# Products of the unit matrix, read by nobody, in TensorE's pauses at three borders of stages

## The reference

```python
x = x + L0_attn(L0_cond(x))    # diagonal state space kernel, 32 heads of causal attention
x = x + L0_ffn(L0_cond2(x))    # low rank adapter per labeler, octonion ternary gate/up/down
x = x + L1_attn(L1_cond(x))    # gathered adapters, 4 heads of sigmoid attention
x = x + L1_ffn(L1_cond2(x))    # top-2 and sparsemax mixtures of rank-16 experts
```

## Time and profile before

| | us |
|---|---|
| median of 3 runs | 2157.1 |
| the runs | 2154.85, 2158.34, 2157.1 |
| the profiled execution | 2158.86 |
| its span, first to last instruction | 2157.1 |
| PE busy | 2108.3 (98%) |
| POOL, DVE, ACT busy | 1255.8, 1338.5, 730.9 |
| mean granted clock of PE | 0.991 |

### The profile page before, as it was taken

The page is one execution under the profiler, slowest core; times in us unless marked ns, Lnnn a source line. Parts: engine busy times, 40 slices in busy tenths (PEclk is TensorE's granted clock), DMA queues, the critical chain, the costliest instruction groups (busy, mean ns, idle before and its releaser), DMA issues. The chain is left out here.

```text
span 2157.1 us, 36235 instructions
## 1 busy us (share of the span) xinstructions
PE 2108.3 (98%) x11876; PEld 1822.5 (84%) x11876; DVE 1338.5 (62%) x2465; ACT 730.9 (34%) x1454; POOL 1255.8 (58%) x1315
## 2 busy tenths in 40 slices
PE   7899999999999998999999999999999999999999
PEld 5788888989888897889898898989887777778887
DVE  7656565665656567665666566566666666654444
ACT  5233232332323233332323233232333645443332
POOL 3587585766758575767758576775844732114220
PEclk9999999999999999999999999999999999999999
DMA  7411112111111210311111211111112200001110
GB/s 238 149 50 40 40 42 65 49 39 39 39 39 40 66 50 30 88 40 40 39 39 39 68 49 39 39 39 39 40 61 78 92 14 0 0 0 40 39 39 19
DMA packets 92036, 107.57 MB, mean 50 GB/s; under 512 B 5569, under 2 KB 71777, under 8 KB 90817
## 3 DMA queue, kind: packets, MB, share of 16 engines
q1 hardware_dynamic: 90689, 102.53, 15.7%
q0 software_dynamic: 1280, 4.20, 0.7%
HBM read 100.79 MB, written 5.94 MB: 49 GB/s over the span
## 5 line engine op out<-in xcount | busy, mean ns | idle before, releaser
L215 PE MATMUL psum<-yc,wh 128*128 128x512 f32 x904 | 363.4, 402 | 9.5 <-DVE yc L1499 5.0
L216 PE MATMUL psum<-yc,wh 128*128 128x512 f32 x904 | 354.6, 392 | 0.0
L217 PE MATMUL psum<-yc,wh 128*128 128x512 f32 x904 | 354.2, 392 | 0.0
L1359 DVE TENSOR_TENSOR resid<-psum,resid 128x512 f32<-128x512 f32 x248 | 171.3, 691 | 148.5 <-PE psum L217 144.3
L215 PE MATMUL psum<-kept,yc 128*128 128x256 f32 x896 | 255.9, 286 | 1.7 <-DVE v_tok L1309 1.0
L941 POOL TENSOR_TENSOR wh<-wh_f,wh 128x256 fp32r<-128x256 f32 x256 | 191.8, 760 | 110.9 <-ACT wh L907 109.0
L217 PE MATMUL psum<-kept,yc 128*128 128x256 f32 x896 | 253.5, 283 | 0.0
L216 PE MATMUL psum<-kept,yc 128*128 128x256 f32 x896 | 253.4, 283 | 0.0
L215 PEld LDWEIGHTS psum<-yc,wh 128*128 128x128 f32 x904 | 171.6, 190 | 43.3 <-DVE yc L1499 5.8
L217 PEld LDWEIGHTS psum<-yc,wh 128*128 128x128 f32 x904 | 170.9, 189 | 36.6
L941 POOL TENSOR_TENSOR wh<-raw,wh 128x256 fp32r<-128x256 f32 x192 | 142.2, 741 | 96.2 <-ACT wh L907 96.2
(11 more groups left out here) (355 smaller groups left out, 4818.5 us busy)
## 6 DMA issues: line engine op xcount, KB each, us to landing
raw<-in_attn_w SPq DMA_DIRECT2D x96, 512.0 KB, 4.8
wo_f<-in_attn_w SPq DMA_DIRECT2D x31, 512.0 KB, 4.0
hankel<-kernel_rows SPq DMA_DIRECT2D x32, 256.0 KB, 4.7
resid<-in_xT SPq DMA_DIRECT2D x4, 1024.0 KB, 9.8
outT<-wide SPq DMA_DIRECT2D x16, 256.0 KB, 2.6
kept_f<-in_l_w SPq DMA_DIRECT2D x3, 1024.0 KB, 5.5
work_f<-in_oct_w SPq DMA_DIRECT2D x4, 680.0 KB, 4.1
resid<-in_xT SPq DMA_DIRECT2D x4, 512.0 KB, 6.1
```

Of the source, the lines that this page charges most:

```text
L215: pe.matmul(out, w[0], x[0], start=start, stop=False)
L216: pe.matmul(out, w[0], x[1], start=False, stop=False)
L217: return pe.matmul(out, w[1], x[0], start=False, stop=stop)
L1359: dve.tensor_tensor(part, psum[:, 5 + (GH + m) % 3, :], part, ALU.add).then_inc(tail_free, 1)
```

## The change

A helper issues `count` float32 products of the unit matrix with the first 256 columns of the constants (themselves never written after their load) into a PSUM bank that nobody reads before it is written anew. Each product is two matmul instructions of 256 columns. It is called six times, at the end of PE's program ahead of a border and at the start of the one behind it: 2 and 5 products at border 1, 2 and 3 at border 2, 2 and 4 at border 3. The first call has a wait ahead of it, for copies of ACT out of the bank that it writes. All else in the diff passes `consts` on.

```diff
+def keep_warm(pe, bank, consts, ident, count):
+
+    for _ in range(count):
+        pe.matmul(bank[:, 0:2 * P], ident, consts[:, 0:2 * P], start=True, stop=True)
...
             convolve(QUARTERS - 1, NCB - 1)
+            pe.wait_ge(comp_copied, 2 * CROWS)
+            keep_warm(pe, psum[:, 6, :], consts, const("ident"), 2)
...
             pe.sem_inc(prod_done, 2)
+            keep_warm(pe, psum[:, 7, :], consts, const("ident"), 5)
             product(0, 0, "P1", fresh=0, start=True)
...
                 for m in range(KC):
                     end_output(i, m)
+            keep_warm(pe, psum[:, 0, :], consts, const("ident"), 2)
...
                 pe.sem_inc(x_used, KC)
+                keep_warm(pe, psum[:, 3, :], consts, const("ident"), 3)
                 with pe.Fori(0, NT) as tile:
...
                     down_product(SLOTS - 2)
                     down_product(SLOTS - 1)
+                keep_warm(pe, psum[:, 2, :], consts, const("ident"), 2)
...
                 pe.sem_inc(x_used, KC)
+                keep_warm(pe, psum[:, 3, :], consts, const("ident"), 4)
                 with pe.Fori(0, NT) as tile:
```

More of the change, by code:

```diff
@@ L240, in build_program @@
         s4d_and_convolution(nc, t, sb, sem, const, consts, resid, psum, kernel_rows, later, hw, v_tok, combos)
-        attention(nc, t, sb, sem, overlaid, const, mm3, resid, psum, kept_raw, kept, hw, v_tok, combos)
+        attention(nc, t, sb, sem, overlaid, const, consts, mm3, resid, psum, kept_raw, kept, hw, v_tok, combos)
         attn.close()
         later["ranks_raw"], later["ranks"] = overlaid(ctx, "ranks", [P, 4, TT])
-        octonion_ffn(nc, t, sb, sem, overlaid, const, mm3, resid, psum, kept_raw, kept, later)
-        layer_one(nc, t, sb, sem, const, mm3, resid, psum, kept_raw, kept, later)
+        octonion_ffn(nc, t, sb, sem, overlaid, const, consts, mm3, resid, psum, kept_raw, kept, later)
+        layer_one(nc, t, sb, sem, const, consts, mm3, resid, psum, kept_raw, kept, later)
+def keep_warm(pe, bank, consts, ident, count):
+    for _ in range(count):
+        pe.matmul(bank[:, 0:2 * P], ident, consts[:, 0:2 * P], start=True, stop=True)
 def wait_apart(engine, semaphore, value, passed):
@@ L971, in load_values, with attention @@
                          .rearrange("g p n -> (g p) n")).then_inc(self.raw_in[p], 16)
-def attention(nc, t, sb, sem, overlaid, const, mm3, resid, psum, kept_raw, kept, hw, v_tok, combos):
+def attention(nc, t, sb, sem, overlaid, const, consts, mm3, resid, psum, kept_raw, kept, hw, v_tok, combos):
     QUADS, HALFTOK = HEADS // 4, 2 * TT
@@ L1790, in gather_adapters, with octonion_ffn @@
                                     ).then_inc(later["gathered"], 16)
-def octonion_ffn(nc, t, sb, sem, overlaid, const, mm3, resid, psum, kept_raw, kept, later):
+def octonion_ffn(nc, t, sb, sem, overlaid, const, consts, mm3, resid, psum, kept_raw, kept, later):
     ctx = ExitStack()
@@ L2357, in _, with layer_one @@
                     down_product(SLOTS - 1)
-def layer_one(nc, t, sb, sem, const, mm3, resid, psum, kept_raw, kept, later):
+                keep_warm(pe, psum[:, 2, :], consts, const("ident"), 2)
+def layer_one(nc, t, sb, sem, const, consts, mm3, resid, psum, kept_raw, kept, later):
     NM = 2
```

## The result

| | kernel before | changed kernel |
|---|---|---|
| median of the runs, us | 2157.6 (2154.85 to 2161.7, 20 runs) | 2154.3 (2153.6 to 2157.4, 20 runs) |
| ratio, 95% interval | | 0.9986 [0.9979, 0.9992] |
| profiled execution (span), us | 2158.86 (2157.1) | 2155.34 (2153.5) |
| mean granted clock | 0.991 | 0.996 |

The change gains 3.3 us, 0.14%; the forecast was 4.95 us. The interval lies clear of 1, but the gain is within the 0.2% that I had called no change.

A forecast was written before the change was run, and what follows sets the result against it. PE, busy 98% of the span, was taken to lose time in pauses and at half clock behind three borders. Gains 1.6 + (1.7 - 0.1) + (2.0 - 0.25) = 4.95 us: median 2157.1 to 2152.2 us, range 2149.0 to 2156.0.

The forecast's parts named there:

- One product, 0.43 us: Each added float32 product of 256 columns on PE: 0.43 us at full clock, 0.86 us at half.
- Products ahead: 0, 0.1, 0 us: Two products ahead of each border delay no result; cost 0, 0.1 and 0 us at borders 1, 2 and 3.
- Products behind: covered at border 1, 0.1 and 0.25 us: Behind border 1 P1's delay is covered by 0.2 us; border 2 costs 0.1 us in all, border 3 0.25 us.
- The clock holds: Falls at borders 2 and 3 gone; border 1 falls in about half of executions, bringing 1.6 us, not 2.3.
- What the falls cost: Half of PE's time with work at half clock behind borders 1, 2, 3: 2.3, 1.7, 2.0 us, together 6.0 us.
- Whether the gain lasts: Attention's POOL chain starts 2.3 us earlier, feed-forward pauses move up with PE, layer one's PE goes on without a pause.
- One border's gain is lost: Rival: one border's 1.7 us of gain is lost, at border 1 or 2; 2154.0 us, chance 0.27.
- The falls come back elsewhere: Rival: the clock falls after the pauses all the same and the added products stay covered; 2157 us, chance 0.10.
- The cover fails: Rival: added products do not hold the clock and run at 0.86 us behind the borders; 2164 us, chance 0.06.
- More is gained: Rival: half of all 17 us at half clock behind the borders is gained, 8.5 us; 2148.6 us, chance 0.05.

The follow-up runs named there:

- the one with more products: Changed kernel with one product fewer ahead of border 2 and products added at attention's turn and in the feed-forward: 2155.9 us.
- kernel with narrow products: Changed kernel with all its added products 2 columns wide in place of 256: 2161.1 us.
- doubled products: Changed kernel with 10, 6 and 8 products behind the borders in place of 5, 3 and 4: 2160.0 us.

## Why the prediction was right, and the term that was off

**One product, 0.43 us.** Right: from the first added product behind a border to the instruction that follows them, 0.41, 0.46 and 0.45 us each at the three borders, and 0.87 us at half clock (3.49 us for four, in the kernel without products ahead).

**Products ahead: 0, 0.1, 0 us.** Right. At border 2 the time from the last real matmul to the border went from 1.34 to 1.44 us.

**Products behind: covered at border 1, 0.1 and 0.25 us.** Right. P6 stands 5.25 us behind border 1, as before, though P1 went from 1.86 to 2.75 us; `base(0)` stands 2.85 us behind border 3 (2.64). PE's first real product stands 1.65 us behind border 2 (1.64).

**The clock holds.** Right, and better than forecast at border 1: I gave the 1.6 us pause a fall in half of the executions. It was 1.5 us, and all four profiles with the changed kernel's products there are at full clock.

**What the falls cost: the term that was mis-sized.** The step that failed is in the sum: the profiled execution is 1.76 us above the median, and I wrote that "the change acts alike on both". It does not, because its falls were long ones: the price read there is more than a median execution has to lose. At border 2 two of five profiles have no fall, so that the mean gain is 0.8 us in place of 1.6. At border 3 the profile that I read had the 6.8 us fall and four of five had 3.4 us: 0.9 us in place of 1.75. At border 1 two of five falls were longer and one was shorter, and 1.9 us came in place of 1.6. So 4.95 us became 3.6 us.

The price of one fall was somewhat high as well. At border 1 the 6.8 us fall costs 1.8 us against the treated mean, forecast 2.3 (the 10.2 us one costs 2.7 us, the 3.4 us one 0.35 us). At border 2 a fall costs 1.35 to 1.5 us; the forecast, less the products' 0.1 us, was 1.6. At border 3 the same 6.8 us gave 1.25 us in place of 1.75, since the wait named below takes its part again.

**Whether the gain lasts.** Right for POOL in attention: L928 starts 8.4 us behind the border, L920 did 10.55 us behind it, 2.1 us nearer, where 2.3 was forecast. Of that 0.3 us is lost at the turn: PE's wait for `wh` ahead of it (841.87 us before, 841.03 after) stands 2.2 us nearer to border 1, its last wait for `qk` behind it (867.84 and 867.32) 1.9 us. In the feed-forward the gain lasted to the stage's end. The forecast was wrong in one place in layer one. I had said that PE goes on without a pause; the rank products come 1.7 us nearer to the border (8.52 against 10.19 us), but behind them PE now waits 0.45 us for DVE's `bound` (the new row above), and 1.25 us of the 1.7 us is left.

**The rivals.** "One border's gain is lost" gave 2154.0 us, nearer to the measured 2154.3 us than my 2152.2 us, but for another reason: no chain ate a whole border's gain, the falls were often shorter than in the profile that I read, or absent. "The falls come back elsewhere" did not come about: no border fell, and the stretches at the turn and in the feed-forward vary between 3.4 and 6.8 us in both kernels. "The cover fails" is what happens at border 3 with products behind it only. "More is gained" failed: by the three stretches of the profile of before (17 us) it would give 8.5 us, where that execution lost 4.9 us to them. The Trainium skill's rule for it ("TensorE: Matmul & The Clock Gate", section "Terms") is an upper bound here, as in parts of the stretches PE waits, and others are hidden behind DVE and POOL.

**Left open.** In the three profiles of the changed kernel the stretch ahead of border 1 is 90.66, 92.33 and 89.80 us, in the three of before 89.28, 89.59 and 89.48 us. The longest of PE's waits in it (8.1 to 9.3 us) is for a DMA, and its differences are as large as a border's gain. With the same products at border 1 it was 89.34 us in the kernel with border 1 alone and 89.45 us in the one with more products, and with none ahead of any border 90.23 us; so the products there need not make it longer. The kernel with narrow products had 96.36 us there. Whether anything of it comes from the change these runs do not settle. Nor do they say why border 2 fell in three profiles and not in two, at pauses of the same length (2.59 us in all five).

No version that was run beats the changed kernel.

## What to carry to other kernels

A fall of the clock costs time only where TensorE sets the pace, and its length and whether it comes at all differ between executions of one program: read it in several profiles of the kernel before you price it. A pause at a border is best filled from both sides, with products of full width that hide under the wait for the other engines: those ahead shorten the pause before the clock can fall, and those behind fill it up to the first real work and not beyond, since each further one is paid nearly in full. Before adding work ahead of a border, look up which engine comes there last.

## What the runs showed of the hardware

- The half-clock stretches behind the borders, at the turn and in the feed-forward came in lengths of 3.4, 6.8 and 10.2 us only, and border 1 showed all three in different executions.
- The length of a pause alone did not decide it: a pause of 1.87 us at border 3 and one of 2.13 us were followed by a fall, pauses of 2.11 and 2.41 us at border 1 (doubled products, products behind only) and, twice, border 2's pause of 2.59 us were not.
- Half clock twice as long cost nothing at the turn, where DVE sets the pace (attention 1540.65 us with 13.6 us of it there, 1540.76 and 1540.95 us with 6.8), but 0.7 to 0.9 us for 3.4 us more of it in the feed-forward.
- Products 2 columns wide did not hold the clock, products 256 wide and transposes 128 wide did (the transposes at two borders of three, in the one execution profiled).
